# Two groups of keys and queries loaded inside the stage that makes them, in a two-layer gated cross-attention kernel

## The reference

```
x = x + tanh(g_xattn[0]) * attention0(layernorm(x), ctx, ctx, mask, wq, bq, wk, bk, wv, bv, wo, bo)
x = x + tanh(g_ffn[0])   * experts0(layernorm(x))       # top-2 of 8 experts, silu, layernorm at the end
x = x + tanh(g_xattn[1]) * attention1(layernorm(x), ctx, q_map, k_map, v_map, output_map)
x = x + tanh(g_ffn[1])   * fp8_linear(x)                # per-tensor scaled e4m3 input and weight, bias
```

## Time and profile before

| what | us |
|---|---|
| median of 3 runs | 1797.37 (1795.66 to 1798.21) |
| the profiled execution, its time | 1793.3 |
| its span, first to last instruction | 1791.5 |
| TensorE busy | 1532.7 |
| VectorE busy | 1272.4 |
| ScalarE busy | 970.8 |
| POOL busy | 661.0 |
| project, from TensorE's start to the last matmul | 23.0 to 134.4 |
| combine, from POOL's first load to TensorE's last matmul | 1171.0 to 1305.1 |

### The profile page before, as it was taken

One profiled execution on the slowest core, in us unless ns is written; L12 is line 12 of the kernel. 1 busy time (PEld: TensorE's weight loads), 2 busy tenths in 40 slices (PEclk: granted clock), 3 DMA queues, 4 the chain that ended last, 5 costly groups with the idle time before them and its releaser, 6 DMA issues. The chain is left out here.

```text
span 1791.5 us, 30430 instructions
## 1 busy us (share of the span) xinstructions
PE 1532.7 (86%) x11934; PEld 1019.2 (57%) x11934; DVE 1272.4 (71%) x1980; ACT 970.8 (54%) x1315; POOL 661.0 (37%) x957
## 2 busy tenths in 40 slices
PE   3882999999989349999999999968838999999865
PEld 2770333333338249999999999934513333333443
DVE  3654899999955766655555554358758999999687
ACT  1540788888854123444454454425516888888545
POOL 1551455555502124433333333243213455444020
PEclk9995899999989569999999999979968999999986
DMA  7557345554543222122132221056573555554102
GB/s 213 183 222 136 83 119 127 125 118 118 113 171 128 71 71 82 44 94 92 43 98 92 74 67 42 31 168 244 194 135 79 124 118 126 124 121 115 41 1 95
DMA packets 116766, 198.71 MB, mean 111 GB/s; under 512 B 28480, under 2 KB 62080, under 8 KB 115600
## 3 DMA queue, kind: packets, MB, share of 16 engines
q1 hardware_dynamic: 82480, 110.20, 20.7%
q0 software_dynamic: 34144, 86.56, 19.0%
HBM read 117.77 MB, written 77.87 MB: 109 GB/s over the span
## 5 line engine op out<-in xcount | busy, mean ns | idle before, releaser
L926 DVE TENSOR_REDUCE a_nmax<-a_ring 128x2 f32<-128x1024 f32 x512 | 608.6, 1219 | 40.8 <-PE a_ring L838 40.1
L908 ACT ACTIVATE a_pexp<-a_ring 128x1024 f32<-128x1024 f32 x512 | 522.6, 1027 | 197.6 <-PE a_ring L848 197.6
L860 PE MATMUL a_pout<-a_pexp,values 128*17 128x256 f32 x4096 | 321.5, 387 | 0.7 <-ACT a_pexp L908 0.7
L838 PE MATMUL a_ring<-a_k,a_q 64*128 64x512 f32 x1024 | 243.9, 474 | 56.1 <-DMA a_q<-qs 45.8
L1536 ACT ACTIVATE e_full<-e_pH,b1T 128x256 f32<-128x256 f32 x320 | 133.8, 469 | 271.0 <-PE e_pH L1496 271.0
L848 PE MATMUL a_ring<-a_q,a_k 64*128 64x512 f32 x1024 | 259.2, 503 | 12.3 <-DMA a_q<-a_nT 9.6
L1565 DVE TENSOR_TENSOR e_hid_lo<-e_full,e_hid_hi 128x512 fp32r<-128x512 f32 x160 | 128.1, 804 | 151.2 <-ACT e_hid_hi L1544 151.2
L848 PEld LDWEIGHTS a_ring<-a_q,a_k 64*128 64x128 f32 x1024 | 96.7, 185 | 234.7 <-DVE a_nmax L926 132.1
L1515 PE MATMUL e_pY<-fc_w_hi,e_hid_hi 128*128 128x256 f32 x640 | 185.0, 289 | 8.9 <-DVE e_hid_lo L1565 8.9
L1496 PE MATMUL e_pH<-e_rowsT_hi,fc_w1T_hi 128*128 128x256 f32 x640 | 182.0, 284 | 1.5 <-DVE e_rowsT_lo L1411 1.5
L1496 PE MATMUL e_pH<-e_rowsT_lo,fc_w1T_hi 128*128 128x256 f32 x640 | 181.8, 284 | 0.0
(11 more groups left out here) (309 smaller groups left out, 2467.4 us busy)
## 6 DMA issues: line engine op xcount, KB each, us to landing
outs<-a_osb SPq DMA_DIRECT2D x64, 256.0 KB, 2.7
fc_raw<-in_L_ffn_fc_w SPq DMA_DIRECT2D x16, 1024.0 KB, 7.0
a_k<-ks POOLq DMA_DIRECT2D x112, 128.0 KB, 3.4
a_q<-qs POOLq DMA_DIRECT2D x112, 128.0 KB, 3.6
BIG<-outs SPq DMA_DIRECT2D x64, 128.0 KB
ytok<-r_zeros SPq DMA_DIRECT2D x8, 1024.0 KB, 9.8
c_yg<-ytok POOLq DMA_DIRECT2D x16, 512.0 KB, 6.8
a_k<-ks POOLq DMA_DIRECT2D x112, 64.0 KB, 3.4
```

The source lines that it names most:

```text
L838: mm = e.matmul(max_bank(m)[:, hh, :], q[j][at, p, t * P:(t + 1) * P], k[j][at, p, :], start=True, stop=True)
L860: mm = e.matmul(pout[n % 2][32 * h:32 * h + VW, at], v[:, b * TPB + t, g * HG + h, :], pexp[t][:, h, at], start=(t == 0 and half == 0), st ...
L908: e.activation(pexp[t][:, 2 * p:2 * p + 2, :], score_bank(n * U + i)[:, :, :], ACT.Exp).then_inc(exped, 1)
L926: e.tensor_reduce(nmax[n % 2][:, :].rearrange("p (x y t) -> p x y t", x=2, y=2)[:, :, p, t], max_bank(m)[:, :, :], AX.X, ALU.max, negate=T ...
```

## The change

- A new class `Inputs` is opened in the project and the combine stage and lives on through the attention. It holds keys and queries of groups 0 and 1, and a `room` of 8 x 1024 values per partition. In the first stage the room holds the stored parts, in the attention the exponentials.
- SP's wait for landing at the end of both stages is gone. ScalarE waits for all stores before its first exponential, POOL before its first load.
- After batches 2 to 5 SP issues half a group's loads (five DMAs) each, so groups 0 and 1 are loaded inside the stage; POOL clears their tiles early in the stage, four memsets. SP waits, before batch 2, for batch 0's stores.
- SP stores the high part when it is there, ahead of the low part.
- The last batch's queries are cut low by VectorE, not POOL (project only).
- In the attention SP loads group 2, writes the first group's maxima, then loads group 3. POOL clears all four tiles of groups 2 and 3. VectorE clears the output banks after the first and the second reduction.
- Normalised tokens and `full` move into the free part of BIG (project); combine's context lies over two weights that are free by then.
- In the last stage four semaphores become one chain, with the same order of work.

```diff
-def store_parts(e, dst, b, parts, count):
+LOADS = 10
+EARLY_GROUPS = 2
+class Inputs:
+    def __init__(self, S, l):
...
+        self.q = [sb(f"q{j}", [P, 2, SEQ], F32R) for j in range(EARLY_GROUPS)]
+        self.k = [sb(f"k{j}", [P, 2, SEQ], F32R) for j in range(EARLY_GROUPS)]
+        self.room = sb("room", [P, 8, KD * SEQ])
...
+    def clear(self, e):
+        for j in range(EARLY_GROUPS):
+            for x in (self.q, self.k):
+                e.memset(x[j][:, :, :].bitcast(F32), 0.0).then_inc(self.blank[j], 1)
...
+    def load_half(self, e, b):
+        if 2 <= b < 2 + 2 * EARLY_GROUPS:
+            n, half = (b - 2) // 2, (b - 2) % 2
+            e.wait_ge(self.blank[n], 2)
+            load_group(self.S, self.l, e, n, self.q[n], self.k[n], self.ld[n], range(half * (LOADS // 2), (half + 1) * (LOADS // 2)))
...
     def store(self, e, b):
+        hi, lo = self.parts[b % self.depth]
+        e.wait_ge(self.high, b + 1)
+        store_part(e, self.dst, b, HI, hi, self.stored[b % self.depth])
         e.wait_ge(self.low, b + 1)
-        store_parts(e, self.dst, b, self.parts[b % self.depth], self.stored[b % self.depth])
+        store_part(e, self.dst, b, LO, lo, self.stored[b % self.depth])
...
              @block.sync
             def _(e):
                 for b in range(B):
+                    if b == 2:
+                        inputs.wait_first_stored(e)
                     k0.store(e, b)
                     q0.store(e, b)
-                k0.wait_stored(e)
-                q0.wait_stored(e)
+                    inputs.load_half(e, b)
...
                     k0.cut_low(e, b)
-                    q0.cut_low(e, b)
+                    if b + 1 < B:
+                        q0.cut_low(e, b)
...
-        pexp = [sb(f"pexp{t}", [P, HG, SEQ]) for t in range(TPB)]
+        pexp = [inputs.room[:, 2 * t:2 * t + 2, :].rearrange("p a (k t) -> p (a k) t", k=KD) for t in range(TPB)]
...
-                for n in range(G):
-                    e.wait_ge(blank[n], 2)
-                    load_group(e, n, ld_first[n])
+                load_first(EARLY_GROUPS)
                 if l == 1:
                     e.dma_start(S.w["wq0"][:, :, :], S.a["L1_ffn_weight"].rearrange("(t p) c -> p t c", p=P)).then_inc(ldw, 16)
                 subtract_maxima(0)
+                for n in range(EARLY_GROUPS + 1, G):
+                    load_first(n)
...
                 k1.store(e, 0)
                 for b in range(B):
+                    if b == 1:
+                        e.wait_ge(inputs.stored_k[0], 64)
+                    if b == 2:
+                        e.wait_ge(inputs.stored_q[0], 64)
                     if b + 1 < B:
                         k1.store(e, b + 1)
                     store_queries(b)
-                for j in range(2):
-                    e.wait_ge(q_stored[j], 64 * (B // 2))
-                k1.wait_stored(e)
+                    inputs.load_half(e, b)
```

More of the change, by code:

```diff
@@ new lines, in load_group @@
+def load_group(S, l, e, n, q, k, count, which):
+    b, g = n // G, n % G
+    at = slice(b * SEQ, (b + 1) * SEQ)
+    lo, hi = CENTRE
+    moves = [(k[lo:hi, :, :], S.key_centre[l][:, at].rearrange("s (o t) -> s o t", o=1).broadcast_to([hi - lo, 2, SEQ])),
+             (q[lo:hi, :, :], S.query_centre[:, :].rearrange("s (o t) -> s o t", o=1).broadcast_to([hi - lo, 2, SEQ]))]
+    for hh in range(2):
+        r, heads = FIRST_ROW[hh], slice(g * HG + hh, (g + 1) * HG, 2)
+        moves += [(k[r:r + 2 * DH, :, :], S.ks[l][heads, 0:2, :, at].rearrange("h s d t -> (s d) h t")),
+                  (q[r + DH:r + 3 * DH, :, :], S.qs[l][heads, 0:2, :, at].rearrange("h s d t -> (s d) h t")),
+                  (k[r + 2 * DH:r + 3 * DH, :, :], S.ks[l][heads, 0, :, at].rearrange("h d t -> d h t")),
+                  (q[r:r + DH, :, :], S.qs[l][heads, 0, :, at].rearrange("h d t -> d h t"))]
+    for m in which:
+        out, src = moves[m]
+        e.dma_start(out.bitcast(F32), src).then_inc(count, 16)
@@ L389, in store_parts, with store_part, __init__ @@
+def store_part(e, dst, b, s, part, count):
     hpt = P // DH
-    for s in range(2):
-        for t in range(KD):
-            e.dma_start(dst[t * hpt:(t + 1) * hpt, s, :, ds(b * SEQ, SEQ)], parts[s][:, t, :].bitcast(F32)).then_inc(count, 16)
+    for t in range(KD):
+        e.dma_start(dst[t * hpt:(t + 1) * hpt, s, :, ds(b * SEQ, SEQ)], part[:, t, :].bitcast(F32)).then_inc(count, 16)
 class Projection:
[L398 to L401, removed]
+    def __init__(self, sem, name, dst, full, parts, stored):
+        self.name, self.dst, self.full, self.parts, self.stored = name, dst, full, parts, stored
+        self.depth = len(parts)
@@ L408, in cut_high @@
             e.wait_ge(self.stored[b % self.depth], 64 * (b // self.depth))
-        e.activation(self.parts[b % self.depth][HI][:, :, :], self.full[:, :, :], ACT.Copy).then_inc(self.high, 1)
+        e.activation(self.parts[b % self.depth][HI], self.full[:, :, :], ACT.Copy).then_inc(self.high, 1)
     def cut_low(self, e, b):
@@ L915, in _ @@
             def _(e):
-                for j in range(G):
-                    e.memset(q[j][:, :, :].bitcast(F32), 0.0).then_inc(blank[j], 1)
-                for j in range(2):
-                    e.memset(pout[j][:, :], 0.0).then_inc(clear, 1)
                 def reduce(m):
@@ L2024, in output @@
                     last.then_inc(yd, 1)
-                e.wait_ge(most, 1)
+                e.wait_ge(factored, MOST)
                 e.transpose(pA[:, :], am[:, :], S.ident[:, :]).then_inc(turned, 1)
                 e.wait_ge(oned, 3)
-                e.wait_ge(factored, 4)
-                e.matmul(pB[:, :], ones[:, :], factor[:, :], start=True, stop=True).then_inc(widened, 1)
+                e.wait_ge(factored, FACTOR)
+                e.matmul(pB[:, :], ones[:, :], factor[:, :], start=True, stop=True).then_inc(turned, 1)
                 turn_rounded(0)
-                e.wait_ge(lifted, 8)
+                e.wait_ge(factored, LIFTED)
                 for b in range(B):
```

171 lines of the change are left out of this document (95 added, 76 removed).

## The result

The changed kernel takes **1767.01 us** (median of 4 runs, 1764.42 to 1771.95), the kernel before 1796.51 beside it (4 runs, 1795.25 to 1798.21): a ratio of 0.9838, 95% interval 0.9813 to 0.9864, 29.5 us less. The forecast was 1776.2 in a range of 1758 to 1788; the rival of free halves stood at 1759.4. The profiled execution took 1765.34, span 1763.1; 28.4 us less span than before.

A forecast was written before the change was run, and what follows sets the result against it. Two boundaries where TensorE idles ahead of the attentions, set by SP's queue, were to give 6.9 + 14.3 = 21.2 us off the median of 1797.37: 1776.2, range 1758 to 1788 for 8 in 10; forecast's chance 0.52.

The forecast's parts named there:

- the rival of free halves: Both boundaries: the queue takes the half loads for nothing, gaining 21.0 and 17.0 us, to 1759.4 us; chance 0.22.
- Wrong if SP's last issue ends at 140 (free halves): First boundary: sign against the forecast, which had SP's last issue end at 153.9.
- the queue would be empty at 147.6 + 12.0 = 159.6: First boundary: four halves at 3.0 us each, 12.0 in all, delay the emptying of SP's queue from 147.6.
- one queue works in order: SP's DMA queue: argument against free halves, beside loads holding the engines 107% busy.
- 5.7 us left at the last issue: Stage end: SP's last issue ends 5.4 to 5.9 us before its full queue is empty, taken as 5.7.
- From start to first score product: Start of the attention: 14 reductions take 17.4 us, with two output bank clears 18.4, and 18.5 to the product.
- the queue is empty at 1319.5: Second boundary: SP's last issue then ends at 1313.8, first score product at 1332.9, 14.3 us earlier.
- The rival of late contexts: Batches' context loads: halves issued just ahead make three land up to 3.0 us later each, 9.0, giving 1785.2; chance 0.16.
- the clock at 0: Start of the attention: TensorE's first ten microseconds of scores stay slow as now, so no gain or loss.
- The clears ahead of POOL's first statistics: Start of the second stage: 3.6 us of POOL clears move the chain behind them by 1.6 us.
- Moved tiles and the chained semaphores: Tiles change no size; the last stage's semaphores set the same waits in another form: 0 (0.2 either way).
- ScalarE's wait for a store at the last high keys: First stage: the cut at 130.31 waits 1.5 us for batch 5's keys to land at 131.8.

The follow-up runs named there:

- its batch's changed kernel: The changed kernel measured again with no edit, in the first batch of runs: 1775.87 us, ratio 0.9804 to the kernel before.
- the changed kernel's third profile: Profile of the changed kernel run unaltered in the third batch, on another chip: 1774.31 us, ratio 0.9813 to the kernel before.
- the last run: Changed kernel plus early load of the exponential's table, last queries' stores issued by ScalarE, and moved clears: 1768.17 us, ratio 0.9788 to the kernel before.

## Why the prediction was right or wrong

The sign and the places were right: both boundaries gave, and by the steps named (loads hidden in the stage, rows no longer late). The time lies 9.2 us under the forecast and 7.6 above the rival of free halves. What the forecast said of the queue did not come: "Wrong if SP's last issue ends at 140 (free halves)" was its own sign, and that issue ended at 141.36 where it had 153.9. That the total was no further off is in part luck, as the errors offset one another at the second boundary.

What came exactly is the part behind TensorE's start: 1.7 us at the first boundary and 3.1 at the second, as the forecast had both, since the rows no longer hold the score product. The part ahead of it was 17.5 and 8.9, forecast 5.1 and 11.2.

**First boundary: 19.2, forecast 6.9.** The step "the queue would be empty at 147.6 + 12.0 = 159.6" failed, in three terms.
- *The half was 1.8 us, not 3.0.* The price came from loads that ran alone at 107% of the engines. Among stores, which hold the engines at 53%, the queue moves more packets while loads are in it. In the changed kernel, first 2 us of stores alone, then with group 2's loads behind them:

```profile
q1 hardware_dynamic: 210, 0.41, 52.3%
...
q1 hardware_dynamic: 334, 0.59, 90.8%
```

  These are 141 to 143 and 147 to 149: 0.59 MB against 0.41, and all on one queue. The forecast held "one queue works in order" against the free halves. It does not follow that the loads add their own time to that of the stores ahead: the trace has both at once. By 1.8 in place of 3.0 the four cost 7.2, 4.8 less.
- *An earlier start of the queue was put at nothing.* The first stores are issued at 44.62, in before at 50.66.

```profile
44.62 5.74 SPq L458 DMA_DIRECT2D ks<-i_room  x4
```

  At 65 us 2.24 MB had been moved and not 1.29, which is 4.6 us at 204 GB/s. Not all of it is the order of the parts. The run with the low part first issues its first stores at 47.28 and has moved 0.22 MB less by 65 than the profile after and 0.53 less than its batch's changed kernel, so the order is 1.1 to 2.6 of the 4.6. The rest may lie in when POOL cuts the first low part, which varies by 3.7 us between runs of the changed first stage (from 44.8 to 48.5; 46.7 in the profile after, 48.3 in before).
- *5.7 us left at the last issue was no constant.* In the profile after, 1.65 MB are issued and not yet moved when SP's last issue ends at 141.36; at the stores' 0.41 MB in 2 us that is 8.0 us, up to 149.4. The forecast took the 1.2 MB of before for a depth that the queue can't pass.

Sum: 147.6 + 7.2 - 4.6 = 150.2 for an empty queue (149.4 by the bytes left); less 8.0 is 142.2 for the last issue (141.36 seen), where the forecast had 153.9. The rival of free halves had TensorE at 140.4 and the score product at 158.9, within 1.8 us of the measured 142.15 and 160.66. Its reason was partly right: the halves are not free (1.8 each), but most of that found room beside the path: TensorE starts 3.9 to 6.2 behind the last high part, of which the path alone takes 3.8.

**From start to first score product: 18.5, measured 18.51.** The 14 reductions and two clears of the earlier trace rows, with the clears between them, as worked out. The run with the clears moved has 17.63, so the clears are 0.9 of it.

**Second boundary: 12.0, forecast 14.3.** Also "the queue is empty at 1319.5" failed: it ran empty from 1292 on, here in 1292 to 1294:

```profile
q1 hardware_dynamic: 21, 0.03, 4.6%
```

The stage ends with its path, and the path is 5.0 longer than the forecast of free halves had it (17.0 for the boundary, where 12.0 came). The last queries start 134.37 after the stage's first context load, in before 130.33: 4.0 later, of which that forecast counted 1.6 for the clears. And they take 2.4 longer. 2.4 and 2.4 are 4.8 of the 5.0.
- *The halves make the stage longer.* Without them the last queries start at 129.88: 4.5 us earlier than here, and 2.8 to 6.6 over the eleven runs with halves and high part first. One way for it shows in TensorE's waits for the context, of this kernel and of the run without halves, for the same batch:

```profile
1236.39 1.97 PE L1036 MATMUL c_pC<-ident,w 128*128 128x128 f32 x8 [3.83 <-DMA w<-in_ctx]
```
```profile
1249.88 1.09 PE L1038 MATMUL c_pC<-ident,w 128*128 128x128 f32 x8 [1.25 <-DMA w<-in_ctx]
```

  Here SP had been issuing a half (1224.25 to 1228.05) when POOL issued the context at 1227.93. TensorE uses it 8.5 us after its issue, without halves 6.6. But this is not the whole: TensorE's waits for contexts from 1195 to 1300 sum to 9.3 us here, 9.8 in before and 6.8 without halves, and the changed kernel's third profile has 6.1, none over 1.93, while its last queries still start at 133.15. That the halves cost the stage these us is shown; that late contexts are the way is shown for single waits only, and the rest is open. The rival of late contexts had 9.0. The forecast had thrown it out by the 169 packets to 7 of the earlier trace rows, and **this is the reading that was wrong**: SP's queue got 7 packets because it was empty. From 1204 to 1218 it had moved 2.1 MB, which is all eight stores of 256 KB that SP had issued for that batch; its timeline, in before:

```profile
1211.20 2.48 SPq L392 DMA_DIRECT2D qs<-c_q_lo  x2
1219.11 1.27 SPq L392 DMA_DIRECT2D ks<-c_parts_k_hi  x2
```

Where both queues have been at work for a while the shares are equal. In before over 109 to 111, SP's stores are issued until 109.53 with 1.2 MB waiting, and POOL's context was issued at 103.57:

```profile
q0 software_dynamic: 74, 0.27, 32.7%
q1 hardware_dynamic: 74, 0.14, 18.3%
```

  By the Trainium skill, "DMA: Bandwidth & Descriptors", section on queues, rings and completion order, each engine alternates between the queues that have work, a packet at a time; the trace agrees in this window, 74 to 74. It doesn't always. In the changed kernel over 1234 to 1236 and in the run without halves over 1248 to 1250 SP had been issuing stores since 1231.30 and 1247.37, and they hardly move while POOL's queue is in full flow:

```profile
q0 software_dynamic: 166, 0.60, 92.7%
q1 hardware_dynamic: 32, 0.05, 8.0%
```
```profile
q0 software_dynamic: 199, 0.73, 99.3%
q1 hardware_dynamic: 3, 0.00, 0.6%
```

  So equal shares can't be counted on either, and why new work comes in so late there isn't shown.
- *TensorE's last queries at the lower clock.* They took 6.09 and not 3.70 (the same eight matmuls), 2.4 us; over 1290 to 1300 the granted clock is 0.67, in before over 1280 to 1300 it was 1.00. Every run with the change or a part of it had it (5.1 to 6.8), the one without halves too (5.84), so late contexts don't explain it, and the cause stays open. The forecast had the clock at 0.

The clears ahead of POOL's first statistics hold the stage back as forecast in kind: the variance stands right behind the fourth clear, where it had idled 1.28.

```profile
1166.60 0.98 POOL L420 MEMSET i_k<- 128x1024 f32 x1
1167.67 0.37 POOL L353 TENSOR_SCALAR c_var<-c_mv 128x4 f32<-128x4 f32 x1
```

Normalised rows start 1.1 later in the stage (21.95 against 20.84), forecast 1.6. Nothing of it is seen at the stage's end: the run without halves has the clears in front too, and its last queries start at 129.88, before has 130.33.

**Terms at nothing.** Low part by VectorE: nothing that shows. Moved tiles and the chained semaphores: nothing that the table of starts lets see, not tried by themselves. The clock at the attention's start stays low, as said: 0.50 over 160 to 170, as the earlier trace rows shows for before.

```profile
160.00:170.00 10.00, 8.79 (x40) 3.46 (x40) 8.21 (x10) 5.12 (x5) 0.00 (x0) 0.50 0.26 48
```

ScalarE's wait for a store at the last high keys did not come (130.60 against 130.31), since the queue was ahead. Missed was the table load, 1.3 us in the second attention: the forecast looked at ScalarE's new wait only for what it waits for, and not for what stands behind it.

**The errors offset one another, at the second boundary.** At the first all went the same way: too dear a half (4.8), an earlier start of the queue that was taken for nothing (4.6) and a queue taken for shallower than it is (2.3) make 11.7, where 12.3 were missing. At the second the queue that was to hold the stage did not, which gave, and what was not in the sum took: the stage's longer way with halves, the clock and the table load, about 8 us. That 12.0 lies near 14.3 there is luck, since the reason for 14.3 did not come. Undoing one part at a time, in ratio to the kernel before: halves 0.0124, the landing wait 0.0082, the order of the stores 0.0016, of the 0.0196 of that batch. Each is uncertain by some 0.004. They add up to more than the whole, as fits parts that each leave another wait in place when the other is missing: loads and landing wait must both be gone before TensorE can start early.

**Open.** That executions have the last high part of queries ready at anything from 133.9 to 139.4 may lie in TensorE's granted clock (1.00 with the earliest, 0.94 with the latest) and in when the stage starts, which itself varies (TensorE's first matmul of the stage from 21.75 in the earliest to 23.76 where the high part was ready at 138.85); neither was tried. What stretches SP's last issues by 0.1 to 2.3 us is open too. Whether the three improvements of the last run are worth 6 us or 3 isn't settled by its intervals.

## What to carry to other kernels

When a queue is seen with few packets beside another's many, look first whether it had anything to move: bytes issued against bytes moved, then shares, and these in more than one window. A price for loads taken where they run alone was too high beside stores, which left the engines half idle here (1.8 us for 3.0); and what a stage's end costs is the later of the queue's last issue and the path of the last data, so both must be worked out and the later one taken. A new wait at the head of an engine's block can push behind it whatever that engine did for nothing while idle, such as a table load: give it one cheap instruction of the kind ahead of the wait.

## What the runs showed of the hardware

- SP's queue held 1.65 MB after the last issue of the first stage (8.0 us at the stores' rate), 1.4 to 1.6 MB in the other runs with four halves, 1.1 in before. No fixed depth shows.
- Stores alone moved 210 packets and 0.41 MB in 2 us at 52.3% of the engines; with a group's loads behind them on the same queue 334 packets and 0.59 MB at 90.8%.
- Four stores' issue takes 3.0 us on an engine whose queue is empty (0.58 to 1.15 each), ten loads' 4.3 us.
- With both queues long at work SP's and POOL's moved 74 and 74 packets in 2 us (before, 109 to 111). Stores issued to SP's queue from 1296.09 with POOL's idle (after) first moved 1.1 us later; issued from 1247.37 with POOL's in full flow (without halves), 3.5 us later.
- The experts and routing between the attentions took 630.5 us on one chip and 640 to 643 on two others, in code that no run changed: about the 12 us by which the kernel before differs between these chips.
